# Order of the first transfers, start-up matmuls and the condition product of an FFN kernel on one core

## The reference, cut to what matters

```
# x [16, 256, 512], cond [16, 256], W3 [256, 512], W2 [512, 512]; all float32
q_emb = relu(cond @ W3 + b3)                       # [16, 512]
v_sum = sum(x, axis=1)                             # over the 256 rows of a batch
y     = (256 * x + v_sum) * q_emb[:, None, :]
hid   = relu(y @ W2 + b2)
hid_q = where(hid > 0.33, 0.5, where(hid < -0.33, -0.5, 0.0))
w     = ternary(weight, 0.2, 0.6) + rram_variation # [512, 512]
out   = x + hid_q @ w.T
```

## Time and profile before

| | us |
|---|---|
| median of 3 runs (176.82 to 177.49) | 176.84 |
| the profiled execution | 176.82 |
| its span, from first to last instruction | 175.0 |
| outside the span | 1.8 |
| PE busy | 170.1 (97%) |
| DVE busy | 114.0 (65%) |
| ACT busy | 61.2 (35%) |
| POOL busy | 23.0 (13%) |

### The profile page before, as it was taken

The page is one execution under the profiler, slowest core; times in us unless marked ns, Lnnn a source line. Parts: engine busy times, 40 slices in busy tenths (PEclk is TensorE's granted clock), DMA queues, the critical chain, the costliest instruction groups (busy, mean ns, idle before and its releaser), DMA issues.

```text
span 175.0 us, 1710 instructions
## 1 busy us (share of the span) xinstructions
PE 170.1 (97%) x556; PEld 119.0 (68%) x556; DVE 114.0 (65%) x133; ACT 61.2 (35%) x161; POOL 23.0 (13%) x24
## 2 busy tenths in 40 slices
PE   7899899999999999999999999999999999999993
PEld 1859898777645478687766655767765755768883
DVE  2527997999989996775379976546173641634333
ACT  2350561994402269678103998501100000000000
POOL 3019400489000720000000000000000000000000
PEclk9999999999999999999999999999999999999999
DMA  5999999999990199995581112121763012113334
GB/s 167 243 257 256 220 218 225 212 258 294 222 191 2 58 353 255 219 336 222 168 311 60 60 60 105 38 101 60 242 237 120 35 54 94 65 60 117 123 148 151
DMA packets 31208, 28.96 MB, mean 165 GB/s; under 512 B 1600, under 2 KB 22368, under 8 KB 31200
## 3 DMA queue, kind: packets, MB, share of 16 engines
q1 hardware_dynamic: 30416, 28.33, 61.3%
q10 hardware_dynamic: 720, 0.52, 1.2%
q0 software_dynamic: 64, 0.00, 0.0%
HBM read 20.47 MB, written 8.39 MB: 165 GB/s over the span
## 4 chain that ended last, share of the span: by engine, by line
PE 87%; DMA 4%; SPq 3%; DVE 2%; ACT 1%; issue 0%
PE out_ps L706 33%; PE hid_ps L740 8%; PE hid_ps L699 6%; PE hid_ps L680 6%; PE hid_ps L672 6%; PE hid_ps L644 6%; PE hid_ps L692 6%; PE hid_ps L637 6%; PE hid_ps L659 6%; PE hid_ps L735 4%; DMA x_in<-in_x 4%; ACT xT L309 1%; DVE xT L368 1%; SPq L211 1%; SPq L209 1%; SPq L181 1%
## 5 line engine op out<-in xcount | busy, mean ns | idle before, releaser
L706 PE MATMUL out_ps<-wT_lo,hid 128*128 128x512 f32 (+1 forms) x128 | 56.7, 444 | 0.0
L706 PE MATMUL out_ps<-wT_hi,hid 128*128 128x512 f32 (+1 forms) x128 | 49.4, 388 | 0.0
L309 ACT ACTIVATE xT<-xT,coef,q_scale 128x256 f32<-128x256 f32 x60 | 31.1, 591 | 9.1 <-DVE coef L402 8.7
L487 DVE SCALAR_TENSOR_TENSOR x_res<-out_ps,x_res 128x512 f32<-128x512 f32 x31 | 21.2, 685 | 19.2 <-PE out_ps L706 19.2
L368 DVE STREAM_TRANSPOSE xT<-x_in 128x1024 f32<-128x1024 f32 x15 | 30.6, 2046 | 4.4 <-DMA x_in<-in_x 4.4
L706 PEld LDWEIGHTS out_ps<-wT_hi,hid 128*128 128x128 f32 x128 | 24.1, 188 | 8.7 <-issue 4.3
L706 PEld LDWEIGHTS out_ps<-wT_lo,hid 128*128 128x128 f32 x128 | 24.1, 188 | 7.6 <-issue 2.2
L320 ACT ACTIVATE junk<-xT,q_emb 128x256 bf16<-128x256 f32 x40 | 19.8, 496 | 20.0 <-DVE xT L368 20.0
L740 PE MATMUL hid_ps<-xT,w_sb 128*128 128x512 f32 x32 | 13.9, 593 | 0.0
L740 PEld LDWEIGHTS hid_ps<-xT,w_sb 128*128 128x128 f32 x32 | 9.8, 309 | 3.6
L699 PE MATMUL hid_ps<-xT,s_mix 128*128 128x512 f32 x24 | 11.3, 595 | 0.0
(11 more groups left out here) (68 smaller groups left out, 168.3 us busy)
## 6 DMA issues: line engine op xcount, KB each, us to landing
x_res<-in_x SPq DMA_DIRECT2D x4, 2048.0 KB, 9.4
out<-x_res SPq DMA_DIRECT2D x31, 256.0 KB, 2.0
x_in<-in_x SPq DMA_DIRECT2D x24, 256.0 KB, 6.9
x_in<-in_x SPq DMA_DIRECT2D x12, 128.0 KB, 5.6
w_sb<-in_L_cond_W SPq DMA_DIRECT2D x5, 256.0 KB, 6.1
x_res<-in_L_ffn_weight SPq DMA_DIRECT2D x4, 256.0 KB, 6.3
x_res<-in_L_ffn_rram_variation SPq DMA_DIRECT2D x4, 256.0 KB, 6.4
w_sb<-in_L_cond_W ACTq DMA_DIRECT2D x1, 256.0 KB, 2.9
```

What stands on the lines that cost most here:

```text
L309: nc.scalar.activation(part, part, ACT.Identity, bias=coef[:, n, k:k + 1], scale=q_scale[:, n, k:k + 1]).then_inc(s_xs, 1)
L487: nc.vector.scalar_tensor_tensor(x_res[:, g % 2, c], out_ps[i % 4][:], SC_X, x_res[:, g % 2, c], ALU.mult, ALU.add).then_inc(s_out, 1)
L706: mm = nc.tensor.matmul(bank[:, cols], hid[:, g % 2, k, c * P:(c + 1) * P], w[:, k, cols], start=(k == 0 and w is wT_lo), stop=(k == KD - ...
```

## The change

Five things, all at the start of the program:

1. Batch 0 is loaded in four transfers of 128 KB, not eight of 64 KB, and these stand ahead of the chunks of W3 on both queues. One semaphore tells of all four, so that the first transpose waits for the whole batch.
2. `WARM` is 14 instead of 7 and `WARM_2` 4 instead of 3; the two fillers inside the condition product are gone.
3. `condT` is [128, 2, 128] instead of [128, 32]: its columns are zeroed by a memset, 16 of 128 are filled, and the product runs over 128 columns for each column group, all into bank `out_ps[0]`. The first 16 columns are read.
4. On SPq batch 1 stands behind two chunks of W2 instead of four. POOL's first sums wait for the second `coef` instead of the first.
5. On DVE `th_col` is made ahead of batch 1, and batch 4 is transposed between the second and the third `quantize` of half 0, not behind the fourth.

```diff
-    WARM, WARM_2 = 7, 3
+    WARM, WARM_2 = 14, 4
-        condT = sbuf("condT", [P, BLK])
+        condT = sbuf("condT", [P, KC, P])
-        q_ps = out_ps[0][:, 0:KD * B].rearrange("p (m b) -> p m b", m=KD)
-        condT_rows = condT[:].rearrange("p (b j) -> p j b", j=KC)
+        q_ps = out_ps[0][:].rearrange("p (m c) -> p m c", m=KD)
...
-        def load_first(engine, half, quads):
-            rows = slice(half * HALF, (half + 1) * HALF)
+        def load_first(engine, quads):
             for q in quads:
-                engine.dma_start(x_in[q * BLK:(q + 1) * BLK, 0, rows], x_split[0, q, :, rows]
-                                 ).then_inc(s_x_first[half], DMA)
+                engine.dma_start(x_in[q * BLK:(q + 1) * BLK, 0, 0:NB], x_split[0, q, :, 0:NB]).then_inc(s_x_first, DMA)
...
             sp.dma_start(cond_in[:], cond_rows).then_inc(s_cond, DMA)
+            load_first(sp, (0, 2))
             sp.dma_start(w3_sb[:, 0], w3_chunks[:, 0]).then_inc(s_w3[0], DMA)
-            load_first(sp, 0, (0, 2))
-            load_first(sp, 1, (0, 2))
-            for k in range(KD):
+            for k in range(2):
                 sp.dma_start(w2_sb[:, k], w2_chunks[:, k]).then_inc(s_w2[k], DMA)
             for q in (0, 2, 1, 3):
                 sp.dma_start(x_in[q * BLK:(q + 1) * BLK, 0, NB:2 * NB],
                              x_split[0, q, :, NB:2 * NB]).then_inc(s_x_in[0], DMA)
+            for k in range(2, KD):
+                sp.dma_start(w2_sb[:, k], w2_chunks[:, k]).then_inc(s_w2[k], DMA)
...
-            pool.wait_ge(s_coef, 1)
+            pool.wait_ge(s_coef, 2)
...
+            load_first(act, (1, 3))
             act.dma_start(w3_sb[:, 1], w3_chunks[:, 1]).then_inc(s_w3[1], DMA)
-            load_first(act, 0, (1, 3))
-            load_first(act, 1, (1, 3))
...
             nc.vector.memset(warm[:], 0.0).then_inc(s_warm, 1)
+            nc.vector.memset(condT[:], 0.0).then_inc(s_condT_zero, 1)
+            dve.wait_ge(s_condT_zero, 1)
             dve.wait_ge(s_cond, DMA)
             for q in range(QUADS):
-                nc.vector.transpose(condT[q * BLK:(q + 1) * BLK], cond_in[:, q * BLK:(q + 1) * BLK]
-                                    ).then_inc(s_condT, 1)
+                nc.vector.transpose(condT[q * BLK:(q + 1) * BLK, :, 0:B].rearrange("p j b -> p b j"),
+                                    cond_in[:, q * BLK:(q + 1) * BLK]).then_inc(s_condT, 1)
             prepare_first()
-            prepare(1)
             dve.wait_ge(s_b2, DMA)
             nc.vector.tensor_scalar(th_col[:], b2_col[:], -1.0, TH_X, ALU.mult, ALU.add).then_inc(s_th, 1)
+            prepare(1)
             prepare(2)
             prepare(3)
             quantize(0, 0)
             quantize(0, 1)
+            transpose_batch(4)
             quantize(0, 2)
             quantize(0, 3)
-            transpose_batch(4)
...
-                    mm = nc.tensor.matmul(q_ps[:, m], chunk_columns(w3_sb[:, k], m), condT_rows[:, k],
+                    mm = nc.tensor.matmul(q_ps[:, m], chunk_columns(w3_sb[:, k], m), condT[:, k],
                                           start=(k == 0), stop=(k == KC - 1))
                 if m == KD - 1:
                     mm.then_inc(s_q_ps, 1)
-                if m % 2 == 1:
-                    nc.tensor.matmul(out_ps[3][:], warm[:, 0:P], warm[:], start=True, stop=True)
```

More of the change, by code:

```diff
@@ L129, in chunk_columns @@
             return w.rearrange("p (c m) -> p m c", m=KD)[:, m]
-        s_x_first = [sem(f"first_batch_loaded{h}") for h in range(2)]
+        s_x_first = sem("first_batch_loaded")
         s_x_second = [sem(f"second_pair_loaded{b}") for b in range(2)]
@@ L143, in adaln_ffn_kernel @@
         s_warm = sem("warm_zeroed")
+        s_condT_zero = sem("cond_transposed_zeroed")
         s_condT = sem("cond_transposed")
@@ L372, in prepare_first @@
             def prepare_first():
+                dve.wait_ge(s_x_first, DMA * QUADS)
                 for h in range(2):
                     cols = slice(h * HALF * BLK, (h + 1) * HALF * BLK)
-                    dve.wait_ge(s_x_first[h], DMA * QUADS)
                     nc.vector.transpose(
@@ L383, in prepare_first @@
                 dve.wait_ge(s_b3, DMA)
-                nc.vector.tensor_tensor(q_emb[:], q_ps.rearrange("p m b -> p b m"),
+                nc.vector.tensor_tensor(q_emb[:], q_ps[:, :, 0:B].rearrange("p m b -> p b m"),
                                         b3_col[:].unsqueeze(1).broadcast_to([P, B, KD]), ALU.add).then_inc(s_q, 1)
```

## The result

The changed kernel takes 177.76 us (median of 16 runs, 177.13 to 178.32) against 176.90 for the kernel before in 16 runs beside them (176.11 to 177.65): ratio 1.0049, 95% interval 1.0031 to 1.0066. It is slower by half a percent, 0.86 us: a small difference, but the interval leaves 1 out. It lies above the range of 175.7 to 177.4. The profiled execution has 177.60 us and a span of 175.8 (175.82), 0.79 us more than the span before (175.03).

A forecast was written before the change was run, and what follows sets the result against it. PE, running without a break from 19.99 us, was taken as the bound; L740 starting at 27.34 instead of 27.67 saves 0.33, the other edits nothing: 176.82 - 0.33 = 176.49, forecast 176.5 us, range 175.7 to 177.4.

The forecast's parts named there:

- The frame: Whole kernel: PE's later work is unchanged, so the time depends on when L740's matmuls start, 27.67 us before.
- P: Start of the condition product on PE, set by the later of W3's landing and the fillers' end: taken as 6.7 us.
- P + 20.64: Start of L740 on PE: condition product's start plus 5.49 to L730, 7.68 for L730 and 7.47 for L735; forecast 27.34 us.
- (a): Landing of W3 behind batch 0, one of two things setting the condition product's start: taken as 6.5 us, bounds 5.9 to 7.5.
- break-even: Start of the condition product at which L740 would start at 27.67 us as before: 7.03 us.
- (b): End of the 14 fillers on PE ahead of the condition product: taken as 6.7 us, bounds 5.8 to 7.1.
- Edits together at nothing: Memset of condT, batch 0's landing near 5 us, and the reordered th_col, POOL sums and batch 4 transpose: together 0 us.
- a sign of error: Observations that would prove the forecast wrong, among them idle PE anywhere after 20 us in the changed profile.
- Path B: Batch 1's path to its matmuls: with two W2 chunks fewer ahead it lands at 12.0, 2.2 us earlier, scaled near 17.8.
- A: Path through the condition product, q_emb and scaling of batch 0 to L730, which starts at P + 5.49 us.
- Rival 2: Start of the program: W3 or fillers late, P = 7.1 to 7.6, a loss of 0.1 to 0.6 us; chance 0.15.
- Rival 3: PE's clock falls back or has not risen before L730, slowing 6 to 12 records: 177.6 to 178.8 us; chance 0.08.

The follow-up runs named there:

- other orders undone: Changed kernel with batch 1 again behind all four W2 chunks, POOL waiting for the first coef, th_col and batch 4's transpose moved back: 177.81 us, ratio 1.0054.
- batch 1 ahead: Kernel before with only batch 1 moved ahead of two chunks of W2 and POOL waiting for the second coef: 177.07 us, ratio 1.0012.
- thin product: Changed kernel with W3 ahead of batch 0 and the condition product over 16 columns again, without the memset of condT: 177.36 us, ratio 1.0021.
- nine fillers: Changed kernel with W3 ahead of batch 0, the memset of condT on POOL, and WARM 9 instead of 14: 177.55 us, ratio 1.0019.
- W3 first: Changed kernel with both chunks of W3 ahead of batch 0 again: 176.50 us, ratio 0.9992.
- fillers only: Kernel before with only the new fillers (14 and 4, none inside the product) and the 128-column condition product: 177.30 us, ratio 1.0042.
- memset on POOL: Changed kernel with the memset of condT on POOL instead of DVE: 177.80 us; with W3 also ahead of batch 0: 176.42 and 176.24 us.
- the changed kernel, third time: Changed kernel run again without any edit: 177.75 us, ratio 1.0066 against the kernel before.

## Why the prediction was wrong

The forecast was 176.5, the result 177.76. By its own steps:

- **The frame** held: everything hung on when L740 could start, and the sum P + 20.64. With the P that was measured, 7.38, it gives 28.02; L738 started at 28.06. L728 started 5.57 behind P (5.49 in the sum), its block took 7.65 (7.68), batch 1's 7.46 (7.47).
- **(a), W3's landing, was mis-sized**: "I take 6.5", and the two chunks landed at 6.6 and 7.29. The upper bound, 7.5, held it. I had put W3 midway between what 290 GB/s would give (5.9) and the row that was the same place in the same queue, batch 0's last landing at 7.0; that row was nearer. In four profiles with this order of transfers W3 landed at 7.05 to 7.29 and the product started at 7.14 to 7.38; in the fifth they are 8.82 and 8.91. That alone turned a gain of 0.33 into a loss of 0.39, since the break-even was 7.03.
- **(b), the fillers**, I took at 6.7; they were over at 6.37 and did not decide. Only in the kernel with the other orders undone did they reach W3's landing. The sentence taken from the Trainium skill (TensorE: Matmul & The Clock Gate, Part 1) on the varying point of the rise agrees with the traces: the rise is recorded at 4.10 to 6.88 us in the profiles with 14 fillers, and the same 14 took 4.61, 4.62, 5.03 and 5.17 us in the profiles shown, and 5.98 in that of the kernel with the other orders undone.
- **"Edits together at nothing" failed.** The memset of `condT` I costed by its own 0.27 us, hidden under the wait for `cond_in`. It was hidden, and it cost 0.40 us none the less, at 56 us, by its place in DVE's stream. The sum had "PE has no wait to lose" there; PE had no slack to lose either. What I named as a sign of error, idle PE anywhere after 20 us, is what came. No rival had it. In the same passage batch 0 was to land "near 5"; it landed at 6.77, and its first transpose began at 6.80, later than the 6.29 of before. That cost nothing, since DVE then still waited 1.80 us for the product.
- **Path B** was early enough, and its figure was met by luck: batch 1 was transposed at 12.09 (forecast 12.0 to 12.1), but it had landed at 11.66 (forecast 12.0), and DVE was busy with `q_emb`, `coef` and `th_col` until then. No wait stood ahead of L733. It was worth nothing, because A was later still; with four chunks of W2 ahead of it (the last experiment) it still would not have been late.
- **Rival 2** (W3 late, P = 7.1 to 7.6) was the case, with 0.15 where it should have had most of the chance; its own price, 0.1 to 0.6, was right for the first half of the loss. Rival 3, the fall of the clock, did not come in the changed kernel's L728, but did in three of the variants (batch 1 ahead, thin product, nine fillers). The range was left by 0.36 us, almost the term that nobody had.

## What to carry to other kernels

Put ahead in the queues what starts the longest chain, and take as its landing time that of whatever stands at the same place in the same queue now, not what the bandwidth would give. A start that hangs on the last of several transfers takes over their scatter (W3 behind batch 0 landed at 7.05 to 8.82 in five profiles, ahead of it at 4.83 to 5.06 in five). A start that hangs on fillers moves with the rise of the clock: 14 of them took 4.61 to 5.98 us.

An instruction on an engine costs its place in the stream too. Where an instruction of one engine releases another with no slack between them (here L466 and L699: a comparison that started 0.40 late cost 0.40), a hidden instruction far ahead can cost more than it lasts. Look in the new trace for "issue" in the chain, check in the engine's own timeline that the engine is idle there (the "0.63 issue" at 50.63 in the changed kernel's chain is no stall: DVE runs L451 then), and move the added instruction to another engine.

Filler matmuls have to reach up to the work that they are for. Removing some because the work ahead is ready earlier can cost more than it gives: five fillers fewer cost 1.3 us in the median (177.55 against 176.24).

## What the runs showed of the hardware that was not expected

- A gap of 0.45 to 0.46 us stands in DVE's stream between the wait ahead of the comparison of L466 and the comparison itself, in every profile with a memset and a wait more on DVE (seven profiles: the changed kernel three times, W3 first, fillers only, other orders undone, and the kernel before with two idle instructions), and in none without them (before, batch 1 ahead, memset on POOL four times, the kernel with nine fillers among them, and thin product). In these last seven the wait behind the comparison comes 0.48 to 0.49 us after the comparison's start, and in the first seven 0.08 to 0.09: the stall is in all fourteen, and only its place differs. One instruction fewer, the memset alone, was enough to put it back behind the comparison. That it belongs to a place in the stream is shown. The place is not one fixed count: among DVE's records the stall stands ahead of the 63rd in the kernel before, and ahead of the 64th with one and with two instructions more. That it comes from the fetching of instructions is my guess and was not tried.
- The granted-clock column reads 1.00 ahead of the first change that a profile records. In the kernel before it says so up to 13 us, where the distances between starts say 1.2 GHz; later falls it does show (0.50).
- The clock fell to 1.2 GHz again after it had risen in five profiles: during the thin product with two fillers inside it (twice, batch 1 ahead at 7.59, and two more DVE instructions at 8.07), in and behind idle time ahead of batch 0's matmuls (thin product, 2.61 us, and nine fillers, 1.71 us), and behind 2.03 us of idle time ahead of the wide product (the changed kernel, third time). The first two have the kernel before's own start, and 27 of the 96 executions of the kernel before in the later sessions have a mean granted clock near 0.98, so it has a source of variation that its profile did not show. These differ from the others of their session by at most 0.3 us in the median, in either direction.
- One `coef` of 128 x 4 took 0.80 us (L402 at 17.47 in the kernel with fillers only) instead of 0.16 to 0.31. Its cause is open.
